# Sixteen-head local attention in a decoder kernel: the opening's order of projections, splits and scatters, and the place of the mask products

## The reference

```python
q, k, v = split_heads(x @ w_qkv.T)            # per batch 16 heads x 128 x 16
scores  = q k^T / sqrt(16), masked to a band of 64 behind each query
out     = softmax(scores) v
x       = x + merge_heads(out) @ w_out.T
```

## Time and profile before

| | us |
|---|---|
| median of 3 runs | 1048.48 |
| lowest, highest | 1046.69, 1048.58 |
| the profiled execution's own time | 1046.12 |
| its span (first to last instruction) | 1044.3 |
| PE, DVE, ACT, POOL busy in the span | 987.1, 772.3, 701.9, 330.7 |

### The profile page before, as it was taken

One profiled execution on the slowest core, in us unless ns is written; L12 is line 12 of the kernel. 1 busy time (PEld: TensorE's weight loads), 2 busy tenths in 40 slices (PEclk: granted clock), 3 DMA queues, 4 the chain that ended last, 5 costly groups with the idle time before them and its releaser, 6 DMA issues. The chain is left out here.

```text
span 1044.3 us, 19330 instructions
## 1 busy us (share of the span) xinstructions
PE 987.1 (95%) x6896; PEld 818.3 (78%) x6925; DVE 772.3 (74%) x1525; ACT 701.9 (67%) x1959; POOL 330.7 (32%) x276
## 2 busy tenths in 40 slices
PE   7999999999999999999999988699999989899997
PEld 3898888888998899889988866577777789774444
DVE  5798867667676676776757989899998644567774
ACT  5888876777767776776662358487788535448882
POOL 1343333322333233323310120054545310106672
PEclk9999999999999999999999998999999999899999
DMA  7322000000000001000205000000000000018652
GB/s 211 94 61 61 1 2 1 2 1 1 2 1 1 1 2 36 2 1 1 82 16 132 1 1 1 1 2 2 1 2 2 2 1 2 8 51 277 217 180 81
DMA packets 31841, 40.21 MB, mean 39 GB/s; under 512 B 8193, under 2 KB 23297, under 8 KB 31745
## 3 DMA queue, kind: packets, MB, share of 16 engines
q1 hardware_dynamic: 31744, 38.98, 11.9%
HBM read 36.74 MB, written 2.23 MB: 37 GB/s over the span
## 5 line engine op out<-in xcount | busy, mean ns | idle before, releaser
L349 POOL TENSOR_TENSOR roped_q<-roped_q,sin_q 128x512 f32<-128x512 f32 x64 | 82.0, 1281 | 302.3 <-DVE sin_q L494 302.3
L1664 ACT ACTIVATE win_P<-banks,win_neg_max 128x128 f32<-128x128 f32 x256 | 91.4, 382 | 27.6 <-DVE win_neg_max L1740 27.3
L349 POOL TENSOR_TENSOR roped_k<-roped_k,sin_k 128x512 f32<-128x512 f32 x64 | 83.2, 1301 | 46.6 <-DVE sin_k L494 46.6
L403 ACT ACTIVATE P<-banks,neg_max 128x128 f32<-128x128 f32 x256 | 90.5, 372 | 6.9 <-DVE neg_max L519 6.6
L437 ACT ACTIVATE oT_hi<-banks,bv_col 128x512 fp32r<-128x512 f32 x64 | 44.1, 690 | 74.2 <-PE banks L667 74.2
L1601 POOL TENSOR_TENSOR win_P<-win_P,win_inv 128x512 f32<-128x512 f32 x64 | 66.9, 1046 | 70.4 <-DVE win_inv L1745 70.3
L412 ACT ACTIVATE sin_k<-banks 64x512 f32<-64x512 f32 x128 | 76.0, 594 | 11.6 <-PE banks L37 10.1
L522 DVE SCALAR_TENSOR_TENSOR oT_lo<-banks,bv_col,oT_hi 128x512 fp32r<-128x512 f32 x64 | 47.9, 749 | 42.6 <-ACT oT_hi L437 42.0
L412 ACT ACTIVATE sin_q<-banks 64x512 f32<-64x512 f32 x128 | 76.0, 594 | 2.9 <-PE banks L37 0.7
L629 PE MATMUL banks<-WO_lo,oT_hi 128*128 128x256 f32 x256 | 72.9, 285 | 0.0
L493 DVE SCALAR_TENSOR_TENSOR roped_k<-banks,qk_bias,cos 128x512 f32<-128x512 f32 x64 | 48.0, 750 | 33.2 <-ACT sin_k L412 33.2
(11 more groups left out here) (428 smaller groups left out, 3141.2 us busy)
## 6 DMA issues: line engine op xcount, KB each, us to landing
ret_V<-moe_gate_rows SPq DMA_DIRECT2D x16, 512.0 KB, 4.8
ctx<-moe_gate_rows SPq DMA_DIRECT2D x16, 512.0 KB, 5.2
X<-in_x SPq DMA_DIRECT2D x4, 512.0 KB, 6.6
stage<-in_wqT SPq DMA_DIRECT2D x4, 512.0 KB, 4.1
stage<-in_wvT SPq DMA_DIRECT2D x4, 512.0 KB, 5.9
stage<-in_woT SPq DMA_DIRECT2D x4, 512.0 KB, 4.3
ctx<-in_ctxT SPq DMA_DIRECT2D x4, 512.0 KB, 5.8
out<-X SPq DMA_DIRECT2D x8, 256.0 KB, 2.4
```

The source lines that it names most:

```text
L349: nc.gpsimd.tensor_tensor(roped[w][:, p, :], roped[w][:, p, :], sin_part[w][:], ALU.add).then_inc(roped_sum[w], 1)
L403: ins = nc.scalar.activation(P[:, i, :], SC[:, i * 128:(i + 1) * 128], ACT.Exp, bias=neg_max[:, r % 2, i:i + 1], accum_out=exp_sum[:, r % ...
L1664: ins = nc.scalar.activation(P[:, h % 2, s, i, :], SC[2 * (h % 2) + s][:, i * 128:(i + 1) * 128], ACT.Exp, bias=neg_max[:, h % 2, at:at + ...
```

## The change

Seven edits, all in `phase_window`. (1) PE projects the first pair's keys ahead of its queries, and ACT rounds them in that order. (2) The first pair's values are projected into the bank `OT`, at once after the queries, where before they went into a `PREP` bank after the split of the queries. The first transposition of pair 1 waits for that split in place of the values' copy. (3) ACT rounds pair 1's transposed x before tick 0, not in tick 1, and DVE splits it in tick 0 after `find_max(0)`. (4) On DVE the splits of keys and queries and `normalise(1)` come ahead of the scatter of batch 4; batches 5, 6, 7 move to ticks 0, 1, 2, batches 8 to 11 to ticks 4 to 7, and 12 to 15 stay at ticks 9, 11, 13, 15. (5) `finish_part(1)` moves from tick 0 to tick 2, `normalise(2)` from tick 2 to tick 3. (6) POOL makes the power of part 1 after the products of tick 1, not before the ticks. (7) In every fourth tick, PE's mask products come ahead of the wait for the pair's queries and keys.

```diff
+        FINISHED = 5, 6, 7, None, 8, 9, 10, 11, None, 12, None, 13, None, 14, None, 15
+        PART_AT = {2: 1, 8: 2, 16: 3}
...
-                for part in range(2):
-                    pool.wait_ge(stat, stat_done[part])
-                    power(PARTS[part]).then_inc(rstd_ready, 1)
+                pool.wait_ge(stat, stat_done[0])
+                power(PARTS[0]).then_inc(rstd_ready, 1)
...
-                    if h in (7, 15):
-                        part = 2 + h // 8
+                    if h in (1, 7, 15):
+                        part = 1 + (h + 1) // 8
...
+                    values = PREP[(i + 1) % 2] if i > 0 else OT
...
+                round_k(0)
                 round_q(0)
-                round_k(0)
                 act.wait_ge(V_cleared, 1)
                 take_v(0)
+                round_xT(1)
...
-                    if p > 0 and m + 1 < PAIRS + CROSS:
+                    if p > 0 and m + 1 < PAIRS + CROSS and h != 1:
...
                 finish_part(0)
+                split_k(0)
+                split_q(0)
+                normalise(1)
                 finish_batch(4)
-                normalise(1)
-                finish_batch(5)
-                split_q(0)
-                finish_batch(6)
-                split_k(0)
...
-                    if p == 1 and m + 1 < PAIRS + CROSS:
+                    if p == 1 and 0 < m < PAIRS + CROSS - 1:
                         split_xT(m + 1)
                     if h < TICKS:
                         find_max(h)
+                    if h == 0:
+                        split_xT(1)
...
-                    if p == 2 and m + 2 < PAIRS + CROSS:
+                    if p == (2 if m > 0 else 3) and m + 2 < PAIRS + CROSS:
                         normalise(m + 2)
-                    if h == 0:
-                        finish_batch(7)
-                        finish_part(1)
-                    if h % 2 == 1 and h < 16:
-                        finish_batch(8 + h // 2)
-                    if h in (8, 16):
-                        finish_part(1 + h // 8)
+                    if h < len(FINISHED) and FINISHED[h]:
+                        finish_batch(FINISHED[h])
+                    if h in PART_AT:
+                        finish_part(PART_AT[h])
...
 # transpose_x
-                    wait(pe, V_ready, i)
+                    if i == 1:
+                        pe.wait_ge(q_lo_ready, 1)
+                    else:
+                        wait(pe, V_ready, i)
...
 # project_v
-                    if i < PAIRS:
+                    if 0 < i < PAIRS:
                         pe.wait_ge(q_lo_ready, i + 1)
...
 # score
+                    wait(pe, exps_done, 2 * (h - 1))
+                    for s in range(2):
+                        nc.tensor.matmul(SC[2 * (h % 2) + s], ident_b[:], flat(band[:]), start=True, stop=True)
                     if h % 4 == 0:
                         pe.wait_ge(q_lo_ready, i + 1)
                         pe.wait_ge(k_lo_ready, 2 * i + 2)
-                    wait(pe, exps_done, 2 * (h - 1))
-                    for s in range(2):
-                        nc.tensor.matmul(SC[2 * (h % 2) + s], ident_b[:], flat(band[:]), start=True, stop=True)
...
+                project_k(0)
                 project_q(0)
-                project_k(0)
                 project_v(0)
```

More of the change, by code:

```diff
@@ L1652, in take_v @@
                     wait(act, weighed, 8 * (i - 1))
+                    values = PREP[(i + 1) % 2] if i > 0 else OT
                     for ql in range(2):
-                        src = PREP[(i + 1) % 2].rearrange("p (h l a d) -> p h l a d", l=2, a=2, d=DH)[:, :, ql]
+                        src = values.rearrange("p (h l a d) -> p h l a d", l=2, a=2, d=DH)[:, :, ql]
                         dst = V[:, i % 2].rearrange("p b (h l a) d -> p (b h) l a d", l=2, a=2)[:, :, ql, :, DH * ql:DH * ql + DH]
@@ L1852, in project_v @@
                 def project_v(i):
-                    if i < PAIRS:
+                    if 0 < i < PAIRS:
                         pe.wait_ge(q_lo_ready, i + 1)
-                    else:
+                    elif i >= PAIRS:
                         pe.wait_ge(cross_q_ready, i - PAIRS + 1)
@@ L1862, in project_v @@
                                 x, weight = (cr_xT_hi[:, i - PAIRS, k, j], cr_xT_lo[:, i - PAIRS, k, j]), (kept["cr_vo_hi"][:, k, :], kept["cr_vo_lo"][:, k, :])
-                            ins = matmul3(nc, PREP[(i + 1) % 2][:, j * D:(j + 1) * D], x, weight, first=(k == 0), last=(k == KD - 1))
+                            ins = matmul3(nc, (PREP[(i + 1) % 2] if i > 0 else OT)[:, j * D:(j + 1) * D], x, weight, first=(k == 0), last=(k == KD - 1))
                     ins.then_inc(v_projected, 1)
```

## The result

| | before | after |
|---|---|---|
| median of 4 runs, us | 1048.53 | 1040.75 |
| lowest, highest | 1046.69, 1048.59 | 1040.40, 1040.93 |
| profiled execution, time and span | 1046.12, 1044.3 | 1040.40, 1038.6 |

The ratio is 0.993, 95% interval 0.9912 to 0.9947. Forecast were 1044.3 us (1041.3 to 1047.2), a gain of 3.3 us from a mean of 1047.5. Of the runs further down, two executions of before (1228.6 and 1230.7 us, mean granted clock 0.75) and one of `both` (2455.6 us, clock 1.00) are in no average or interval here, and no run explains them.

A forecast was written before the change was run, and what follows sets the result against it. The prediction took DVE's queue to bound the local attention until tick 16 and PE later; 1.8 us (opening) plus 1.5 (masks) gave 3.3 off a mean of 1047.5, so 1044.2, rounded to 1044.3, range 1041.3 to 1047.2.

The forecast's parts named there:

- Masks, 1.5 us: Ticks 20, 24, 28: mask products ahead of the wait bring scores 0.5 us earlier each, 1.5 us in all.
- Opening, 1.8 us: Stage start to tick 8: fewer DVE holes less added collisions, a gain of 1.8 us that stays to tick 16.
- the 2.46 us of holes: DVE's idle up to tick 8 falls from 4.34 to 1.88 us, a gain of 2.46.
- the new hole before the k split: DVE waits 1.3 us before `split_k(0)` in the opening, where it started a scatter before.
- The collisions: Up to tick 8, DVE scatters beside POOL's products lose 2.6 us, where 2.0 were lost before.
- B: Rival: opening gives nothing, only masks do, through late keys or collisions of 2.5; gain 1.5 or less, 1046.0; 0.24 with D.
- rival D: Ticks 0 to 3: more short pauses lower PE's clock, roughly doubling its work; ends as B, counted in B's 0.24.
- is closed: From the opening to tick 16, DVE's queue has no idle but some 0.64 us per pair before the add.
- Rival A: PE's chain sets the end: opening and all seven mask stalls pay, at most 8.9 us, likely 6, giving 1041.5; chance 0.14.
- C: Rival: ticks 0 to 6, scatters and products block each other, 4.9 us lost, slower by 0.9, 1048.4; chance 0.08.

The follow-up runs named there:

- both: Changed kernel with each tick's scatter ahead of the tick's second inversion, and the scatter of batch 4 ahead of `split_k(0)`; median 1039.06 us.
- after_again: The changed kernel run once more with no edit; ratio to the kernel before 0.993 again.
- before_filled: The kernel before with 16 filler matmuls added, 8 ahead of the first values and 8 in tick 1; 0.32% faster.
- masks_only: The kernel before with only the mask products moved ahead of the wait in every fourth tick; gained 0.53%.
- opening_only: The changed kernel with the mask products put back behind the wait in every fourth tick; gained 0.52%.

## Why the prediction was wrong

- What bounds each part of the stage: right for the profile it was read from. DVE to tick 16, PE after it, and the masks' gain at ticks 20, 24, 28.
- Masks, 1.5 us: right, 1.43.
- Opening, 1.8 us: 1.4 between the two first profiles (tick 8 at 48.0 for 49.4), 2.4 with after_again's, whose clock in the first 8 us was before's 0.79. The nearness hides two errors. Of the 2.46 us of holes that the sum takes away, the 1.25 before `find_max(2)` were the clock's, since before_filled loses them without any new order; and the new hole before the k split was 1.79, 1.64 and 0.96 for 1.3, by the clock at which the keys are projected. The collisions were well priced: 2.7 us for the 2.6 forecast (3 x 0.73 and 0.49).
- The step that failed is the clock, "I count it there", as a part of B and rival D. It was taken as a risk of the new order, worth nothing otherwise, when it was the weakness of the old one. The one profile of before had it at 0.63 from 680 to 684; another execution had 0.50 from 672 to 684 and 0.56 to 688 and lost 3.3 us more, while all three profiles of the changed kernel have 1.00 there. The rows had the pauses of 1.2 and 2.3 us and the queries at half rate behind them, and the sum gives them no price in time, because DVE's queue "is closed" over them. What the runs showed in its place: 69 executions of before at a mean clock of 0.9812 and 15 of the changed kernel at 0.9865, which is worth 2.6 us by before's line, over 3.2 us at equal clock.
- That these 3.2 (or 3.6 at 0.987) lie near the sum's 3.3 is luck in part. By the same count masks_only lies 2.9 us under before's line where its stage term is 1.4, opening_only 1.6, and the two together would make 4.5.
- The second half of the same fault: the profiled execution was 2.4 us faster than the median, which the forecast averaged away as noise. Its time and its clock, 0.982, lie near before's line (1046.6 there), on which 1048.5 us would go with 0.978; the slower executions hold more half clock than this profile showed.
- Rival A gave a figure nearer to the result (1041.5) for a reason that the profiles refute: PE's mask products of tick 2 came 4.9 us earlier in the stage, and its end only 2.9. D had the right quantity with the wrong sign, and B's condition came true (keys late by the lower clock) without its result. C fell: of its six scatters four collided, each in one half, and lost 0.5 to 0.7 us.

What stays open: in which part of the execution the clock's share of the gain lies. In the five profiles of the two kernels the stage averages 177.1 us before and 172.2 after, 4.9 of the 5.8 us. The code ahead of it took 661.7 and 659.7 us before, 660.8, 660.8 and 663.3 after, and the code behind it 207.1 and 207.0 before, 205.3, 207.2 and 206.8 after, so no difference is shown there. Five profiles are few against a spread of 7 us between executions of one kernel. Open too is why the clock fell in some executions behind the same pauses and not in others.

## What to carry to other kernels

A stretch in which PE pauses for one or two microseconds several times has two prices, the pause and the chance that the clock falls behind it. The second may be the larger, shows in only some executions, and looks in a timeline like a wait for a late input. Where a profiled execution is faster than the median, look for the pattern that it doesn't show before summing from it, and compare two profiles only where the granted clock in the stretch is the same. Work moved into a pause (a mask product, even a filler) can pay more than its own length. And a queue that gets ahead can open a pause on the next engine, whose clock then takes the gain back.

## What the hardware showed unexpectedly

Sixteen added matmuls made the kernel 0.32% faster, and without six of them the changed kernel's ratio was 0.9973 instead of 0.9946. Executions of the one kernel before ranged from 1043.4 to 1050.7 us, and the mean granted clock, 0.974 to 0.987, goes with most of that (correlation -0.91 over 69 executions). One pause of 1.2 us on PE stood ahead of a fall to 0.52 in a stretch where three profiles without it had 1.00. A DVE instruction with two inputs in SBUF waited out the GpSimd product that had started before it (1.15 us for 0.43), and ran at 0.43 in all 14 places once no product was under way.
